# A state-space and mixture block on one core: product sums carried to TensorE's turn instead of joined on GpSimd, with a re-timed order

## The reference, cut to what matters

```
xz = x @ W_in.T;  xc, z = split(xz)
u = silu(causal_conv4(xc) + b_c)
dt, B, C = split(u @ W_x.T);  delta = softplus(dt @ W_dt.T + b_dt)
h[t,d,n] = exp(delta[t,d]*A[d,n]) * h[t-1,d,n] + delta[t,d]*B[t,n]*u[t,d]
y[t,d] = sum_n h[t,d,n]*C[t,n] + u[t,d]*D[d]
out = (y * silu(z)) @ W_out.T
```

## Time and profile before

| what | us |
|---|---|
| median of three runs | 7707.89 |
| lowest and highest | 7706.72, 7708.32 |
| the profiled execution, its own time | 7704.26 |
| its span, first to last instruction | 7702.5 |
| DVE busy in the span | 7066.7 (92%) |
| PE busy (ends modelled) | 7011.1 (91%) |
| POOL busy | 6663.3 (87%) |
| ACT busy | 6029.3 (78%) |

### The profile page before, as it was taken

One profiled execution on the slowest core, in us unless ns is written; L12 is line 12 of the kernel. 1 busy time (PEld: TensorE's weight loads), 2 busy tenths in 40 slices (PEclk: granted clock), 3 DMA queues, 4 the chain that ended last, 5 costly groups with the idle time before them and its releaser, 6 DMA issues. The chain is left out here.

```text
span 7702.5 us, 98947 instructions
## 1 busy us (share of the span) xinstructions
PE 7011.1 (91%) x29580; PEld 3860.8 (50%) x29580; DVE 7066.7 (92%) x6228; ACT 6029.3 (78%) x13267; POOL 6663.3 (87%) x3115
## 2 busy tenths in 40 slices
PE   7899999999999999999999999999999999987799
PEld 3444544544554454544554555444554544444664
DVE  5999999999999999999999999999999999999755
ACT  7788888888788888877888888777888887776564
POOL 5999999999999999999999999999999999998010
PEclk9999999999999999999999999999999999998999
DMA  3222222222222222222222222222222222221765
GB/s 107 77 85 84 79 85 72 79 85 81 86 78 86 78 73 83 83 87 70 87 88 69 76 69 77 73 75 70 75 77 68 76 71 73 76 72 52 257 229 183
DMA packets 282695, 684.05 MB, mean 89 GB/s; under 512 B 37872, under 2 KB 38128, under 8 KB 254384
## 3 DMA queue, kind: packets, MB, share of 16 engines
q1 hardware_dynamic: 252464, 626.31, 24.7%
q10 hardware_dynamic: 29696, 51.40, 1.8%
HBM read 508.76 MB, written 168.82 MB: 88 GB/s over the span
## 5 line engine op out<-in xcount | busy, mean ns | idle before, releaser
L1172 POOL TENSOR_TENSOR bu<-w,b_rep 128x1022 f32<-128x1022 f32 x2048 | 4797.9, 2361 | 416.6 <-DVE h L1289 413.1
L1289 DVE TENSOR_TENSOR_SCAN h<-decay,bu 128x1024 f32<-128x1024 f32 x2048 | 4644.0, 2277 | 216.0 <-ACT decay L928 71.0
L666 PEld LDWEIGHTS turn<-ident_m,h 128*128 128x128 f32 x16384 | 1963.2, 143 | 2697.1 <-issue 1287.4
L928 ACT ACTIVATE decay<-delta,neg_a 128x511 f32<-128x511 f32 x4096 | 2664.9, 684 | 738.8 <-DVE h L1289 735.6
L666 PE MATMUL turn<-ident_m,h 128*128 128x128 f32 x16384 | 2550.5, 280 | 489.5 <-DVE acc L1319 352.2
L1319 DVE SCALAR_TENSOR_TENSOR acc<-turn,c_now,acc 128x512 f32<-128x512 f32 x2816 | 1966.5, 733 | 139.8 <-PE turn L666 138.8
L1214 POOL TENSOR_TENSOR prod<-prod 128x1024 f32<-128x1024 f32 x448 | 1060.5, 2367 | 10.1 <-ACT prod L958 10.1
L588 PE MATMUL proj<-conv_in,conv_diag 128*128 128x512 f32 x1984 | 995.4, 601 | 67.6 <-ACT halo L818 67.6
L588 PE MATMUL proj<-x_conv,w_in 128*128 128x512 f32 x2048 | 1034.4, 602 | 9.3 <-ACT u L825 8.1
L588 PE MATMUL proj<-x_gate,w_in 128*128 128x512 f32 x2048 | 1012.4, 594 | 0.0
L958 ACT ACTIVATE prod<-turn,c_now 128x512 f32<-128x512 f32 x1024 | 696.3, 683 | 317.4 <-PE turn L666 296.5
(11 more groups left out here) (167 smaller groups left out, 5721.6 us busy)
## 6 DMA issues: line engine op xcount, KB each, us to landing
b_rep<-b_rows SPq DMA_DIRECT2D x1024, 256.0 KB, 3.2
u_rows<-u SPq DMA_DIRECT2D x64, 1024.0 KB, 4.3
u_back<-u_rows SPq DMA_DIRECT2D x256, 256.0 KB, 3.5
x_gate<-xt SPq DMA_DIRECT2D x32, 1024.0 KB, 7.7
xt<-stage ACTq DMA_DIRECT2D x128, 256.0 KB, 2.4
x_conv<-xt SPq DMA_DIRECT2D x31, 1024.0 KB, 6.3
x_gate<-in_x_dram SPq DMA_DIRECT2D x16, 1024.0 KB, 5.1
x_l<-in_x_dram SPq DMA_DIRECT2D x16, 1024.0 KB, 10.0
```

Of the source, the lines that this page charges most:

```text
L666: mm = pe.transpose(out[:, b * P:(b + 1) * P], h[:, (G * GROUPS + k) % H_RING, b, j * P:(j + 1) * P], ident[:])
L928: act.activation(decay[:, (G * SLOTS_BODY + s) % DEC_RING, 1:T], delta[:, blk, 1:T], ACT.Exp, scale=neg_a[:, n, blk:blk + 1]).then_inc(dec ...
L1172: pool.tensor_tensor(bu[:, (G * PAIRS + s // 2) % BU_RING, :, 1:T], w[:, blk:blk + 2, 1:T], b_rep[:, g % B_RING, 1:T].unsqueeze(1).to_broa ...
L1289: dve.tensor_tensor_scan(h[:, (G * GROUPS + k) % H_RING, 2 * pr:2 * pr + 2, :].rearrange("p b t -> p (b t)"), decay[:, at:at + 2, :].rearr ...
```

## The change

The joins go. `turn_y` adds the products itself: behind the four transposes of `acc` come two more, of the half's total in `prod`, one for each of its two tiles, so a y tile has six. ACT's tiles are now j = 3 of an even state and j = 0 of the next (`V_AT = (3, 0)`): both of one pair, in slots 8m + 8 and 8m + 9. Each half has a buffer for its first pair and total, and all others share one (`SPARE`), so a product waits until the pair just before is added. A half's first product waits for the half's last y tile. All sums come after `inputs` of p = 4q + 9. The y tiles move to slots 116, 118, 121, 124 and 16, 24, 32, 40. Order, takes and silus move: silu_u to slots 46 and 62, silu_z to 110 and 126; takes of out0 66, out1 72, x_proj 79; norm0 starts in 58, norm1 77, norm2 79, norm3 81; conv1's start in 14 now has its take in 14.

```diff
-         ('conv_half', 7, 0), ('conv', 6, 0), ('conv', 7, 0), ('norm', 0, 0), ('out', 0, 0), ('norm', 1, 8),
-         ('out', 1, 0), ('x_proj', 0, 0), ('norm', 2, 0), ('norm', 3, 0), ('turn_c', 0, 0), ('delta_next', 0, 0),
-         ('delta_next', 1, 0), ('out', 2, 0), ('delta_next', 2, 0), ...
+         ('conv_half', 7, 0), ('conv', 6, 0), ('conv', 7, 0), ('norm', 0, 0), ('out', 0, 0), ('out', 1, 0),
+         ('x_proj', 0, 0), ('norm', 1, 0), ('turn_c', 0, 0), ('delta_next', 0, 0), ('norm', 2, 0),
+         ('delta_next', 1, 0), ('norm', 3, 0), ('out', 2, 0), ('delta_next', 2, 0), ...
-TAKE_LATER = {('out', 0): -1, ('gate', 0): 1, ('gate', 2): 2, ('turn_c', 0): -1, ('conv', 5): -1, ('delta', 5): -1}
-SILU_LATER = (6, 6, 4, 4)
-V_SUM_AT = (10, 10, 10, 10, 10, 10, 10, 9, 9, 9, 10, 10, 10, 10, 10, 9)
-JOIN_AT = (41, 72)
+TAKE_LATER = {('conv_half', 1): -1, ('conv_half', 2): -1, ('out', 0): 0, ('norm', 0): -1, ('gate', 0): 1, ('gate', 2): 2,
+              ('turn_c', 0): -1, ('conv', 5): -1, ('delta', 5): -1}
+SILU_LATER = (8, 2, 1, 0)
+V_SUM_AT = 9
-Y_AT = ((116, 118, 122, 124), (20, 28, 36, 44))
+Y_AT = ((116, 118, 121, 124), (16, 24, 32, 40))
 ...
-WEIGHT = {..., "state": 0.55, "y": 1.6}
+WEIGHT = {..., "state": 0.55, "y": 1.9}
-V_AT = (0, 3)
-V_BUFFER = (0, 1, 2, 1, 2, 1, 2, 1, 2, 1, 0, 1, 0, 1, 0, 1)
+V_AT = (3, 0)
+SPARE = 2
+V_BUFFER = tuple(q // HALF_Q if q % HALF_Q == 0 else SPARE for q in range(GROUPS // 2))
 ...
 def emptied_before(q):
-    old = max(o for o in range(-len(V_BUFFER), q) if V_BUFFER[o] == V_BUFFER[q])
-    ...
+    old = q - 1 if (q - 1) % HALF_Q else q - 2
+    return "pair", old % (GROUPS // 2)
 ...
-            pe.wait_ge(vsum_set, joined)
+            pe.wait_ge(x_done, summed)
             for j in range(J):
-                mm = pe.matmul(out[:, j * P:(j + 1) * P], acc[:, hf, j, b * P:(b + 1) * P], ident[:], start=False, stop=j == J - 1,
+                pe.matmul(out[:, j * P:(j + 1) * P], acc[:, hf, j, b * P:(b + 1) * P], ident[:], start=False, stop=False,
+                          is_transpose=True)
+            pe.wait_ge(vsum_set, added)
+            for odd in range(2):
+                j = V_AT[odd]
+                mm = pe.matmul(out[:, j * P:(j + 1) * P], prod[:, hf, odd, b * P:(b + 1) * P], ident[:], start=False, stop=odd == 1,
                                is_transpose=True)
 ...
+            if k % 2 == 0 and q % HALF_Q == 0 and not kind.first:
+                old = "y", q // HALF_Q, HB - 1
+                behind = TURN_TILES if q == 0 else 0
+                act.wait_ge(turn_full, turn_base(G, kind) + (ALL_TURNS.index[old] + 1 - behind))
+            if k % 2 == 0 and q % HALF_Q and not (kind.first and q == 1):
+                act.wait_ge(vsum_set, sum_base(G, kind) + (kind.sums.index(emptied_before(q)) + 1 + C_PROD))
 ...
-        def join(G, kind, op):
-            ...
-            pool.tensor_tensor(both, both, prod[:, V_BUFFER[hf * HALF_Q]], ALU.add).then_inc(vsum_set, 1)
```

More of the change, by code:

```diff
@@ L109 @@
 TURN_AT, CARRIED = turn_tiles()
-WEIGHT = {"x_proj": 1.1, "delta": 1.25, "delta_next": 1.25, "turn_c": 0.5, "norm": 0.5, "state": 0.55, "y": 1.6}
+WEIGHT = {"x_proj": 1.1, "delta": 1.25, "delta_next": 1.25, "turn_c": 0.5, "norm": 0.5, "state": 0.55, "y": 1.9}
 def timetable():
@@ L1253, in body @@
                 for op in SUM_AT[p]:
-                    if op in kind.sums and op[0] == "pair":
+                    if op in kind.sums:
                         add_pair(G, kind, op)
-                    if op in kind.sums and op[0] == "join":
-                        join(G, kind, op)
         all_chunks(pool, body)
@@ L1261, in _ @@
         for op in SUMS_CARRIED:
-            if op[0] == "pair":
-                add_pair(G_END, end, op)
-            else:
-                join(G_END, end, op)
+            add_pair(G_END, end, op)
     @block.vector
```

51 lines of the change are left out of this document (21 added, 30 removed).

## The result

The changed kernel takes **7811.7 us** (median of 4 runs, 7804.8 to 7816.1) against 7708.1 for the kernel before on the same chip (4 runs): ratio 1.0133 [1.0117, 1.0149], **slower by 104 us**. The forecast was 7615, its range 7545 to 7715.

The account below looks back on a forecast made before the run. It took DVE's idle time as all there was to win or lose; its terms summed to -2.4 us in 18 chunks and -3.3 in 14, 89 us off the profiled 7704.3, which lies 3.6 below the median: 7615, range 7545 to 7715.

Parts of the forecast that it names:

- What bounds it: Whole chunk: DVE's work stays the same, so only its idle time, 8.3 us or some 13 a chunk, can change.
- The joins: nothing.: POOL: two joins of 2.35 us a chunk leave, but they are off the path, so nothing is gained.
- Two more transposes: PE, each y tile: 2.1 us of PE a chunk, of which 0.3 shows (bounds 0 and 2.1).
- The silu of slot 68, the order.: DVE stalls go: 2.28 us (2.90 in 14 chunks) behind the silu, 0.74 and 0.98 at conv takes, 2.08 in 14.
- the norms' 1.4 us: Normalizing chunks: norm2 and norm3 wait behind slot 82's products, norm sums stand between those of 10 and 11; bounds 0 to 4.
- Keep their distance to the gap: nothing.: silu_u at slot 46 and silu_z at 110 and 126: their moves cost nothing.
- One buffer: ACT's products wait for POOL's pair sum: 1.0 us a chunk (bounds 0 and 8), 1.5 where the chunk normalizes.
- The step that failed: New waits set against the stalls that go, giving -2.4 us in each of 18 chunks and -3.3 in each of 14.
- Wrong if the period of the second layer is above 217.2: Sign against the forecast: a second-layer chunk taking longer than its 217.2 us before the change.
- The other: Sign against the forecast: the stretch from the scan of slot 84 to that of 112 becoming longer by over 2 us.
- The slower one: Rival: ACT's uncovered waits for sums at p = 49, 53, 57 and 61 add 8 us a chunk; 7795, chance 0.14.
- A wash: Rival: stalls that go return one wait further, at slot 46 to 47; 7704 or so, chance 0.10.

Follow-up runs that it names:

- e4: The kernel before without its two joins a chunk and nothing in their place (product sums missing from y): 7705.1 us, ratio 0.9996.
- e3: The changed kernel with four transposes in a y tile, the two added ones left out (product sums missing from y): 7790.0 us, ratio 1.0107.
- i1: The changed kernel's places with the sums of the kernel before (joins, three buffers in turn, second half's y tiles at 20 to 44): 7799.7 us, ratio 1.0116.
- e2: The changed kernel with each pair sum one pair of slots earlier on POOL: 7789.7 us, ratio 1.0108.
- e1: The changed kernel with the third y tile of the first half back in slot 122: 7807.1 us, ratio 1.0132.
- h1: The kernel before with ScalarE's two tiles of a pair of states taken as in the changed kernel, nothing else: 8057.7 us, ratio 1.0457.
- f1: The changed kernel with norm 1 before the second output tile, norm 2 before x_proj and norm 3 before turn_c: 7807.7 us, ratio 1.0129.
- f3: The changed kernel with norms ordered as in f1, the third y tile at slot 122 and conv6's taps at slot 48: 7771.8 us, ratio 1.0083.
- g9: The kernel before, joins kept, with g1's places where chunks don't normalize; elsewhere second silu_u at 62, takes of out0 at 66, norm1 at 67: 7604.1 us, ratio 0.9867.
- g1: The kernel before, two conv_half takes one slot earlier, first output tile and norm 1 two later, norm 2 before x_proj: 7660.4 us, ratio 0.9937.
- e6: e1 with four products of the identity added in each of slots 122 to 126: 7760.2 us, ratio 1.0071.
- j1: f3 with e6's products of the identity added: 7786.8 us, ratio 1.0099.

## Why the prediction was wrong, point by point

- **What bounds it** held: DVE's idle time is where all versions differ. DVE's work in a second-layer chunk is 209.0 us before and 209.7 after.
- **The joins: nothing.** Right, shown by e4 and by POOL's idle time, which grew by 7.5 us a chunk, about the joins' 4.7 and what the chunk had lengthened by.
- **Two more transposes.** 0.3 us a chunk said, 0.7 measured by e3's median and 0.4 between the profiled executions, inside the bounds. Two of them in a y tile follow at 0.11 us each (from 5021.23 to the next turn at 5021.45, where the row's 0.38 us runs to the modelled end of the second). The Trainium skill's 275 ns ("TensorE: Matmul & The Clock Gate", Part 4) agrees with the mean of one float32 transpose here, 279 ns in the row of L667 above, and not with the pitch in a run; the 0.6 estimated from it was no farther from the cost than the 0.3.
- **The silu of slot 68, the order.** The gains were right: 68, 78, 15 and 23 all went. What stood in their place was not: the norms' 1.4 us came out as 4.1 at slots 82 and 83, beyond the bounds of 0 to 4, and the first output tile's wait for a bank in slot 59 (1.55) was not in the sum.
- **"Keep their distance to the gap: nothing."** True of the silus' places by themselves: i1 has the silu and the taps in slot 46 and no stall at 48. Of the 0.97 us in the changed kernel's second layer 0.61 go when the pair sums come earlier (e2), so most of it belongs to the next term; i1's conv tiles stand elsewhere too, and the rest is not shown.
- **One buffer.** The forecast looked for POOL's lag at p = 49 to 61 only and took POOL to be ahead elsewhere. ACT waits for a pair sum there, 6.4 us in slots 98, 106 and 114 of a chunk of the second layer, but 1.72 us at slot 42 and 0.60 at 58 too. On DVE the stretch from slot 84 to 116 grew from 53.9 to 54.8 us, the 1.0 that was said (2.1 against i1), and the 0.6 us or more at slot 48 come on top.
- **The step that failed** is the list of what stands in the stalls' place. The forecast priced the new waits at 1.6 us in a chunk of the second layer and 4.2 in one that normalizes. In the second layer 9.2 us came: 2.8 at 11, 19, 51, 75 and 91, 2.9 at 99, 106, 107 and 115, 2.0 at 121, 1.0 at 48, and 0.6 at 2, 3 and 43. Of DVE's waits of before 7.7 us went, where 4.0 had been said, and its own work took 0.7 longer. So -2.4 became +2.3, and -3.3 became +4.5 where the chunk normalizes (4.1 at 82 and 83, 1.6 at 59). The diff moves ScalarE's tiles by four slots, and against them every take, silu and y tile; of those only what had been a stall was costed. The y tile's move from 122 to 121 stood in the diff with no sentence at all: 2.0 us at slot 121, 31 times, 63 us in all by the trace, though e1 shows that mending it alone gives back only 4.6. h1 prices the shift with nothing moved after it: 352 us.
- **Its own signs.** "Wrong if the period of the second layer is above 217.2" came true (219.6). The other did not: from the scan of slot 84 to that of 112 it is 1.7 us longer (46.9 to 48.6, start to start; the forecast's 44.6 counts from the end of the first), under the 2 us that it had named.
- **The rivals.** The slower one gave 7795, near the result by luck: it wanted 8 us a chunk of DVE's time from the held buffer. ACT did wait 8.7 us for it in the second layer and 6.2 where the chunk normalizes, but DVE felt 3 to 4 of them, and its other losses were not in that rival. A wash came nearest in kind ("found again one wait further"), but stopped at break-even. 0.14 for slower was too low, since none of the cases held "the new places are worse than the old".
- Not settled: how the 104 us divide between places and sums, since i1 has stalls of its own, and what makes the waits behind ScalarE's pairs. e1, f1 and f3 mend three of the larger waits, and 40 us are got where 119 were summed.

## What to carry to other kernels

When a change shifts one periodic user of a shared engine, list every operation that sits at a fixed distance to it and cost each new neighbourhood, the ones that never stalled included; the stalls of before only tell where the old places were bad. A buffer taken from a ring is priced at every slot where its user comes, not only where its filler is known to lag. A long operation on an in-order engine (here 4.5 us) has three things to keep clear of: the two halves of anything that holds all buffers of a ring, the issue that the bottleneck needs next, and the take that frees another ring. And before the arithmetic is reshaped to take load off an engine with idle time in front of its critical stretch, try to mend the stalls with the old arithmetic: g9's 1.3% were there without the change.

## What the hardware did that was not expected

- TensorE's granted clock fell to the lower of its two levels, mostly for 3 to 7 us, after stretches in which PE had little to do. In g1 it fell when PE had stood still for 4.8 us. At the turn of the chunk PE had only tiles to turn: e1's window with PE busy 3.75 of 7 us was followed by one at 0.65 of full clock, in which four transposes took 1.12 us, not 0.60, and four products 3.16, not 1.88. With that gap filled by products of the identity 37 of 39 dips and 47 us were gone (e6), eleven of them at slot 82, where nothing was filled. In f3 the same filling took the dips at the turn of the chunk away, brought more at slots 80 to 95, and cost 15 us (j1). An engine off the bound can thus be too idle.
- A dummy 128x128 product costs 0.118 us of PE in a run (2.84 us for 24), with a 128-column moving side. PEld was busy 6.03 of 7 us in e6's window, so the weight loads may be what sets that pace; no run tests it.
